# Second layer eight experts at a time, with a ring of 24 activation tiles and five shared banks

## The reference, cut to what matters

```
t = tokens of x + attention(layernorm(x))            # 2048 tokens, 64 channels
xf = layernorm(t)
top_w, top_i = top_k(xf @ Wg + bg, 2); top_w = softmax(top_w)
w_dense = one_hot(top_i) weighted with top_w, summed  # 2048 x 8
for e in range(8):
    h = gelu(xf @ W1[e] + b1[e])                      # hidden size 256
    out += w_dense[:, e:e+1] * (h @ W2[e] + b2[e])
result = t + out
```

## Time and profile before

| | |
|---|---|
| runs | 123.01, 123.14, 121.89 us; median 123.01 |
| profiled execution | 122.06 us; its span in the trace 120.3 us |
| TensorE matmuls | 115.6 us busy, 96% of the span |
| TensorE weight loads | 85.7 us, 71% (beside the matmuls) |
| VectorE | 78.6 us, 65% |
| ScalarE | 70.0 us, 58% |
| GpSimd | 33.4 us, 28% |
| granted TensorE clock | 1.00 over the whole span |

### The profile page before, as it was taken

The page is one execution under the profiler, slowest core; times in us unless marked ns, Lnnn a source line. Parts: engine busy times, 40 slices in busy tenths (PEclk is TensorE's granted clock), DMA queues, the critical chain, the costliest instruction groups (busy, mean ns, idle before and its releaser), DMA issues.

```text
span 120.3 us, 3332 instructions
## 1 busy us (share of the span) xinstructions
PE 115.6 (96%) x1282; PEld 85.7 (71%) x1282; DVE 78.6 (65%) x267; ACT 70.0 (58%) x134; POOL 33.4 (28%) x51
## 2 busy tenths in 40 slices
PE   6999999999999889999999999999999999999990
PEld 5489956777888688969766876766766667666660
DVE  0489595843869989988990089977319064096972
ACT  4338799030696164578891994691963919739200
POOL 6637999991000003033340040000000000000370
PEclk9999999999999999999999999999999999999999
DMA  3679500000000000000000059911089780001001
GB/s 100 180 182 224 159 8 0 5 5 5 0 0 5 0 3 0 0 5 0 0 3 0 11 173 246 237 46 44 11 242 230 212 220 16 0 0 54 0 0 46
DMA packets 5460, 8.05 MB, mean 67 GB/s; under 512 B 1412, under 2 KB 3908, under 8 KB 5444
## 3 DMA queue, kind: packets, MB, share of 16 engines
q1 hardware_dynamic: 5344, 7.80, 25.3%
q10 hardware_dynamic: 100, 0.03, 0.2%
HBM read 7.24 MB, written 0.59 MB: 65 GB/s over the span
## 4 chain that ended last, share of the span: by engine, by line
PE 83%; DVE 9%; ACT 2%; issue 2%; POOL 1%; POOLq 1%; DVEq 0%
PE PS L996 36%; PE PS L1293 18%; PE PS L1112 13%; PE PS L1071 2%; DVE HEADWISE L898 2%; PE PS L1178 2%; PE PS L1081 2%; PE PS L1008 2%; PE PS L1217 1%; PE PS L1094 1%; PE PS L1203 1%; POOL XP L449 1%; PE PS L1024 1%; DVE XB L717 1%; PE PS L1248 1%
## 5 line engine op out<-in xcount | busy, mean ns | idle before, releaser
L573 ACT ACTIVATE MS<-PS,B 128x512 f32<-128x512 f32 x48 | 29.1, 690 | 7.2 <-PE PS L996 7.0
L996 PE MATMUL PS<-XS,W1H 128*128 128x512 f32 x64 | 26.6, 415 | 0.0
L996 PE MATMUL PS<-XS,W1L 128*128 128x512 f32 x64 | 25.3, 395 | 0.0
L1293 PE MATMUL PS<-MS,W 128*64 128x256 f32 x192 | 22.3, 383 | 0.0
L874 DVE SCALAR_TENSOR_TENSOR WY<-PS,B,HEADWISE 128x256 f32<-128x256 f32 x24 | 10.5, 480 | 14.8 <-PE PS L1293 14.4
L1293 PEld LDWEIGHTS PS<-MS,W 128*64 128x64 f32 x192 | 13.2, 137 | 8.5 <-ACT MS L573 1.5
L996 PEld LDWEIGHTS PS<-XS,W1H 128*128 128x128 f32 x64 | 12.0, 188 | 4.9 <-ACT MS L573 1.0
L1112 PE MATMUL PS<-HEADWISE,BANDS 32*32 32x448 f32 (+2 forms) x480 | 15.3, 564 | 0.0
L449 POOL TENSOR_TENSOR XP<-XP,WY 128x256 f32<-128x256 f32 x4 | 3.2, 808 | 41.1 <-DVE WY L924 40.8
L1112 PEld LDWEIGHTS PS<-HEADWISE,BANDS 32*32 32x32 f32 x480 | 10.3, 103 | 4.5 <-issue 1.5
L996 PEld LDWEIGHTS PS<-XS,W1L 128*128 128x128 f32 x64 | 12.1, 188 | 1.8
(11 more groups left out here) (135 smaller groups left out, 182.5 us busy)
## 6 DMA issues: line engine op xcount, KB each, us to landing
HEADWISE<-spread_dram SPq DMA_DIRECT2D x14, 256.0 KB, 5.0
W<-in_w_dram SPq DMA_DIRECT2D x3, 512.0 KB, 7.9
X<-in_x_dram SPq DMA_DIRECT2D x2, 256.0 KB, 3.2
HEADWISE<-spread_dram SPq DMA_DIRECT2D x4, 128.0 KB, 3.1
out_dram<-XP SPq DMA_DIRECT2D x4, 128.0 KB, 2.4
W<-spread_dram SPq DMA_DIRECT2D x2, 256.0 KB, 6.0
VEC<-in_vectors_dram SPq DMA_DIRECT2D x1, 132.0 KB
WQ<-in_w_qkv_dram SPq DMA_DIRECT2D x2, 48.0 KB, 3.0
```

Of the source, the lines that this page charges most:

```text
L573: act.activation(hidden(n), PS[:, h_bank(n), :], ACT.Gelu, bias=B1[:, k:k + 1]).then_inc(gelu_done, 1)
L996: return pe.matmul(PS[0:parts, bank, cols[0]:cols[1]], lhsT, rhs, start=start, stop=stop)
L1293: i = pe.matmul(PS[C * b:C * b + C, bank, at:end], W2[:, KC * e + k, :], hidden(KC * (E * s + e) + k)[:, N * b:N * b + N], start=begins an ...
```

## The change

Four edits. On TensorE each pair's second layer is done for all eight experts in one stretch: S(0, 0 to 7) behind F(1, 0 to 3), S(1, ...) behind F(2, 0 to 3), S(2, ...) behind F(3, 0 to 3), and S(3, ...) at the end. F(0, 7) moves ahead of tokens(0), and gelu(0, 7) ahead of read_tokens(0) and copy_xs(3). The ring gets 24 places, six of the new ones in MSQ and two in BANDS. Bank 5 is no longer the tokens' own: after the first six tiles, hidden tiles and turned tokens take the bank that has been free longest, of 0, 1, 6, 7 and, from tokens(0) on, 5; each waits for the user that had it before.

```diff
-        HRING, IN_MS = 16, 12
-        SIZE_H, SIZE_W = (HRING - IN_MS) * PT, 2 * E * N
+        HRING, IN_MS, IN_HEADWISE, IN_MSQ = 24, 12, 4, 6
+        SIZE_H, SIZE_W = IN_HEADWISE * PT, 2 * E * N
...
         def hidden(n):
             slot = n % HRING
-            return MS[:, :, :].rearrange("p j c -> p (j c)")[:, PT * slot:PT * slot + PT] if slot < IN_MS \
-                else hidden_more[:, slot - IN_MS, :]
+            if slot < IN_MS:
+                return MS[:, :, :].rearrange("p j c -> p (j c)")[:, PT * slot:PT * slot + PT]
+            if slot < IN_MS + IN_HEADWISE:
+                return hidden_more[:, slot - IN_MS, :]
+            if slot < IN_MS + IN_HEADWISE + IN_MSQ:
+                return MSQ[:, :, :, :, :, :].rearrange("p s q h x i -> p (s q h x i)")\
+                    [:, PT * (slot - IN_MS - IN_HEADWISE):PT * (slot - IN_MS - IN_HEADWISE) + PT]
+            return BANDS[:, :, :].rearrange("p d t -> p (d t)")\
+                [:, PT * (slot - IN_MS - IN_HEADWISE - IN_MSQ):PT * (slot - IN_MS - IN_HEADWISE - IN_MSQ) + PT]
...
-        Y_BANKS, LAST_Y_BANKS = (2, 3, 4), (2, 3, 4, 5, 6, 7, 0, 1)
+        Y_BANKS = (2, 3, 4)
...
+        def banks_in_turn():
+            users, tiles = [], iter(range(KC * E * PAIRS))
+            for count, tokens_next in ((E, 0), (QUAD, 1), (QUAD, 2), (E, 3), (E, None)):
+                users += [("h", next(tiles)) for _ in range(KC * count)] + ([("t", tokens_next)] if tokens_next is not None else [])
+            bank_of, user_before, last_user, used = {}, {}, {}, list(H_MANY)
+            for user in users:
+                if user[0] == "h" and user[1] < FEW:
+                    bank_of[user] = H_FEW[user[1] % 2]
+                    user_before[user] = last_user.get(bank_of[user])
+                    last_user[bank_of[user]] = user
+                    continue
+                bank = TOKEN_BANK if user == ("t", 0) else used[0]
+                bank_of[user], user_before[user] = bank, last_user.get(bank)
+                last_user[bank] = user
+                used = [b for b in used if b != bank] + [bank]
+            return bank_of, user_before, last_user, used
+
+        BANK_OF, USER_BEFORE, LAST_USER, FREE_FIRST = banks_in_turn()
+        LAST_Y_BANKS = Y_BANKS + tuple(FREE_FIRST)
+
         def h_bank(n):
-            return H_FEW[n % 2] if n < FEW else H_MANY[(n - FEW) % 4]
-
-        def h_before(n):
-            return max((m for m in range(n) if h_bank(m) == h_bank(n)), default=None)
+            return BANK_OF["h", n]
+
+        def wait_bank_read(pe, user):
+            if user is not None:
+                kind, n = user
+                pe.wait_ge(gelu_done if kind == "h" else tokens_read, n + 1)
...
             gelu(0, 6)
+            gelu(0, 7)
             read_tokens(0)
             copy_xs(3)
-            gelu(0, 7)
...
             def tokens(s):
+                bank = BANK_OF["t", s]
                 if s == 0:
                     pe.wait_ge(b_read[PAIRS - 1], B_PROJ)
-                else:
-                    pe.wait_ge(tokens_read, s)
+                wait_bank_read(pe, USER_BEFORE["t", s])
...
-                    if h_before(n) is not None:
-                        pe.wait_ge(gelu_done, h_before(n) + 1)
-                    elif h_bank(n) == 0:
+                    wait_bank_read(pe, USER_BEFORE["h", n])
+                    if USER_BEFORE["h", n] is None and h_bank(n) == 0:
                         pe.wait_ge(a_read[1], A_XT)
...
-                    elif bank == TOKEN_BANK:
-                        pe.wait_ge(tokens_read, PAIRS)
                     else:
-                        pe.wait_ge(gelu_done, KC * E * PAIRS - 4 + LAST_Y_BANKS.index(bank) - 4 + 1)
+                        wait_bank_read(pe, LAST_USER[bank])
...
             first_layer(0, 6)
-            for e in range(QUAD):
-                second_layer(0, e)
+            first_layer(0, 7)
             tokens(0)
             xt(3)
-            first_layer(0, 7)
             first_layer(1, 0)
             gate(1)
             for e in range(1, QUAD):
                 first_layer(1, e)
-            for e in range(QUAD, E):
+            for e in range(E):
                 second_layer(0, e)
             tokens(1)
             for e in range(QUAD, E):
                 first_layer(1, e)
-            for e in range(QUAD):
-                second_layer(1, e)
             for s in (2, 3):
                 tokens(s)
                 for e in range(QUAD):
                     first_layer(s, e)
-                for e in range(QUAD, E):
+                for e in range(E):
                     second_layer(s - 1, e)
                 for e in range(QUAD, E):
                     first_layer(s, e)
-                if s == 2:
-                    for e in range(QUAD):
-                        second_layer(s, e)
             for e in range(E):
                 second_layer(PAIRS - 1, e)
```

More of the change, by code:

```diff
@@ L562, in read_tokens @@
                 if s % OF_PART == 0:
-                    act.activation(WT[:, s // OF_PART, :], PS[0:2 * OF_PART * E, TOKEN_BANK, N:2 * N], ACT.Copy)\
+                    act.activation(WT[:, s // OF_PART, :], PS[0:2 * OF_PART * E, BANK_OF["t", s], N:2 * N], ACT.Copy)\
                         .then_inc(wt_read, 1)
-                act.activation(outs[:, s, :], PS[:, TOKEN_BANK, 0:N], ACT.Copy).then_inc(tokens_read, 1)
+                act.activation(outs[:, s, :], PS[:, BANK_OF["t", s], 0:N], ACT.Copy).then_inc(tokens_read, 1)
             def gelu(s, e):
@@ L1244, in tokens @@
                     for half in range(2):
-                        pe.transpose(PS[0:2 * OF_PART * E, TOKEN_BANK, N + 128 * half:N + 128 * half + 128],
+                        pe.transpose(PS[0:2 * OF_PART * E, bank, N + 128 * half:N + 128 * half + 128],
                                      WDN[:, half, s:s + OF_PART].rearrange("p s b e -> p (s b e)"), IDT[:, :])
                 for half in range(2):
-                    i = pe.transpose(PS[:, TOKEN_BANK, 128 * half:128 * half + 128],
+                    i = pe.transpose(PS[:, bank, 128 * half:128 * half + 128],
                                      X2[:, 2 * s + half].rearrange("p b c -> p (b c)"), IDT[:, :])
```

## The result

The changed kernel takes 123.32 us (median of 22 runs, 122.65 to 124.10), the kernel before 122.46 in the same comparison (22 runs, 121.85 to 123.34): ratio 1.0083, 95% interval 1.0060 to 1.0107. By the ratio that is 1.02 us slower (0.86 by the two medians); the forecast was 1.05 slower. The profiled execution took 122.85 us with a span of 121.0, against 122.06 and 120.3. Its part ahead of the experts happened to be 0.19 us quicker, so I compare from one fixed place to another inside the trace: from the start of first_layer(0, 4), which is 59.00 us before and 58.81 after, to the start of the last second layer, 110.50 and 111.21. It is 51.50 us before and 52.41 after (worked out before rounding), **+0.91 us**. Behind it the closing chain is the same, 9.8 us in both.

What follows compares the result with a forecast made beforehand. The prediction took TensorE to bound the kernel from 60 to 110 us. Its terms, -0.73 + 1.12 + 0.66 = +1.05 us, on the 123.01 us median of the runs gave 124.06, stated as 124.0 us, range 122.3 to 125.0.

Steps and rivals of the forecast that it cites:

- Term 1: TensorE's second layer: seven stretches become four, saving the cost of entering and leaving three; -0.73 us.
- Term 2: Near 65 us: TensorE's gate(1) waits for ScalarE's late copy_xs(3), with small waits and a restart; +1.12 us.
- Term 3: Two runs of sixteen first-layer tiles: late tiles wait for GELUs to free banks, with restarts; +0.66 us.
- (b): ScalarE behind 60 us: GELU pace is 0.60 us a tile, so waits grow to +1.7, 124.7 us; chance 0.24.
- (c): At gate(1): no wait, as the copies come earlier; 122.9 us, or 122.3 without bank waits; chance 0.16.
- (d): TensorE's second-layer stretches: the seams are not saved, matmul records being partly modelled; 124.8 us, chance 0.08.
- (e): Tiles behind the gate: the clock falls to 1.2 GHz after the new idle time; 126.9 us, chance 0.04.
- The ring and the banks: GELU places and hidden-tile banks: the ring of 24 adds no wait, the new places 0 to 0.02 us a tile.
- the six result slots: Second-layer results: six slots suffice for four pairs in a row, VectorE staying just ahead of TensorE; no cost.

Runs made afterwards that it cites:

- e4: Changed kernel with the first merge alone undone (second layer of pair 0 in two parts, read_tokens(0) and copy_xs(3) ahead of gelu(0, 7)); ratio 1.0043 to the kernel before.
- e7: Changed kernel with six banks for hidden tiles and tokens, and gate(1) moved behind first_layer(1, 2); ratio 0.9981 to the kernel before.
- e6: Changed kernel with bank 4 given to hidden tiles from tokens(1) on (six banks), leaving two for second-layer results; ratio 1.0024 to the kernel before.
- e3: Changed kernel with bank 5 kept for the tokens, so four banks for the hidden tiles; ratio 1.0201 to the kernel before.
- e1: Changed kernel with gate(1) moved two experts later on TensorE, behind first_layer(1, 2); ratio 1.0024 to the kernel before.
- e8: Kernel before with three more stretches of second layer, first and second layer changing over every two experts in pairs 2 and 3; ratio 1.0073 to the kernel before.
- e2: Changed kernel's ring of 24 and five shared banks, with the kernel before's order on TensorE and ScalarE; ratio 1.0021 to the kernel before.
- e9: Changed kernel with the first merge undone and six banks for hidden tiles and tokens; ratio 1.0082 to the kernel before.
- e5: Changed kernel with ScalarE's copy_xs(3) put ahead of read_tokens(0), TensorE's order unchanged; ratio 1.0055 to the kernel before.

## Why the prediction was right

**What bounds.** TensorE from 59 us on, with the others mattering through waits alone. For every kernel but e4 the interval in time holds the difference that the distance shows. The forecast was given as 124.0 us and 123.32 was measured: most of the 0.68 between them is the base, 123.01 from three runs where 22 runs gave 122.46.

**Term 1, the seams.** Forecast -0.73 us, measured -0.82. The first merge saves 0.24: two entries and stretches take 7.86 us before (61.65 to 65.58 and 71.80 to 75.72), and one entry and stretch with the straight way from first layer to the turning take 7.62 after (69.00 to 76.39, and 0.23). The two later ones save 0.58 (e7). The excess is mostly in one turning, that of tokens(3), which the forecast took to be free of the order. The transposes and the way to the next tile take 0.20 us where second layer is ahead of them (the kernel before) and 0.13 where first layer is (e7):

```profile
98.86 0.44 PE L1248 MATMUL PS<-IDT,HEADWISE 128*128 128x128 f32 x2
99.05 0.48 PE L996 MATMUL PS<-XS,W1H 128*128 128x512 f32 x1
```

```profile
94.91 0.38 PE L1280 MATMUL PS<-IDT,HEADWISE 128*128 128x128 f32 x2
95.05 0.48 PE L1026 MATMUL PS<-XS,W1H 128*128 128x512 f32 x1
```

The two stretches, 7.06 for twice 3.60, came out as worked.

**Term 2, the gate.** Forecast +1.12 us. The distance to tokens(1) grew from 16.72 to 17.58, and with the 0.24 that the first merge saves the term is +1.10. The idle time was 0.84 and not 0.95: TensorE came to the gate as worked out (64.62, which is 64.8 less the 0.19 by which this execution was ahead), but from GELU 12 to the first copy ScalarE needed 2.28 us in place of 2.34, and 1.10 for the three copies in place of 1.12. The rest, 0.26 in place of 0.17, is small waits of tiles 14 and 15 (0.14) and of xt(3) (0.06), and a gate that took 0.89 behind its wait and not 0.80 (each rounded).

**Term 3, the long runs.** Forecast +0.66 us, measured +0.63 (e6). Here the number was luckier than the working. ScalarE in the changed kernel:

```profile
77.33 4.73 ACT L603 ACTIVATE MS<-PS,B 128x512 f32<-128x512 f32 x8
81.90 0.35 ACT L593 ACTIVATE WT<-PS 32x256 f32<-32x256 f32 x1
```

Eight GELUs from 77.33 to 81.90 are 0.571 us each, and four from 61.99 to 64.27 are 0.570. In the kernel before the starts inside both runs of eight lie 0.57 us apart as well. The forecast took 0.577, from (4.74 - 0.70) / 7; but the last GELU of that row lasted 0.73, and the last of the other (4.66) 0.67, so both rows say 0.57. The same slip made the 2.34 of term 2. With 0.57 the forecast's own bounds (0.4 at 0.566, 0.66 at 0.577) would give about 0.5 us, an estimate. On the other side it had five or six places of waiting with a restart of 0.05, and there are eight, four tiles in the second half of each run. Of the 0.63 us only 0.18 is late starts of those tiles' first matmuls; 0.46 lies between their first and second ones, 0.27 to 0.31 us apart in place of 0.233 (each rounded). The mechanism (late tiles held by the bank five users before) is what e3 and e6 show; the split of its cost is not what was forecast.

**Sum.** -0.82 + 1.10 + 0.63 = +0.91 us, as the trace has it, where the runs give +1.02; the forecast was +1.05. The misses of the terms (0.09, 0.02 and 0.03) are small and all in one direction.

**The rivals.** (b), a pace of 0.60: it did not come, GELUs started 0.57 us apart in every run of the changed kernel, 0.59 only from the first to the second behind an idle. The 0.59 at 62.19 that spoke for it was read with the same slip: 1.30 less 0.73 is 0.57. (c), no wait at gate(1): the timeline and e1 refute it. (d), seams not saved: e8 refutes it in time, e7 in the trace. (e), the clock: 1.00 in the stretches from 60 to 110 us, through an idle of 0.84 us and the small ones at the banks. The Trainium skill ("TensorE: Matmul & The Clock Gate", section "A second HAM failure mode: psum-queue depth-cycling") warns of short idles between groups while banks are cycled; here they were there, and the clock stayed, so nothing of the 126.9 us that the prediction puts on (e) came. In e3, where nearly every late tile waits, it stayed at 1.00 too, from 60 to 110 us.

The ring and the banks, costed at nothing, cost nothing (e2), and the six result slots made no wait in the new order, whose stretches took 7.06 us each. That count was worked out for this order alone, and e9 shows how narrow it is with four slots in another.

## What to carry to other kernels

When a block of work is moved on the bounding engine, ask which engine drained its backlog behind it: the seams saved were worth 0.82 us, and one copy that now came too late behind two GELUs took 0.84 back, while moving its consumer two experts later returned it. Longer runs of one kind need buffers in proportion to the difference of the two paces (0.467 against 0.57 us a tile: six banks were enough for sixteen tiles, and five cost 0.63 us). And before a buffer is taken from another use, look for the earliest point at which that use falls behind, not its steady state. Take a pace from starts: the length of a merged row less a guessed last instruction was off by 0.007 us a tile here.

## What the runs showed of the hardware

A wait costs more than its idle time. Gate(1) started 0.09 and 0.10 us behind the end of the copy that released it (changed kernel, e5), and then took 0.89 us in place of 0.80. The loss is at its first matmul, 0.10 us to the second in place of 0.03. Its first weight load starts 0.03 us ahead of it there (65.43) and 0.23 ahead in e1 (67.04), so a load that could not run ahead is the likely reason; no run tests it by itself.

GELUs of 128x512 start 0.57 us apart in a run, whether one of them lasts 0.66 or 0.81 us (both in the changed kernel, from 82.42 and from 97.61). The pitch sets the pace, and the end of a GELU frees its bank: the weight load of each of the eight waiting tiles came 0.05 or 0.11 us behind such an end, or behind that of a copy.

Going from the first layer's kind of matmul to the second layer's and back cost 0.34 us a stretch in e8, with no engine waited for and the clock at 1.00; what in the engine takes that time was not tried.
